# The router's mask, broadcast from its rows on chip, and an earlier transpose in the head of an audio tower

## What is computed

```python
h = gelu(x[:, 1:] @ W[:C] + x[:, :1] @ W[C:] + b)          # [16, 374, 256]
y = layernorm(h)
h = h + y + softmax(y @ y.T / max(|y| |y'|, 1e-8)) @ y      # first norm, "rows 1"
z = layernorm(h)                                            # second norm, "rows 2"
logits = unit(z) @ unit_columns(sim) - sigmoid(gates)       # 8 experts
mask = logits > 0, or the two best experts of a token that has none
w = softmax over the masked experts of relu(logits)
q, k, v = sum_e mask[t, e] * (z @ proj[e])                  # proj: [8, 256, 128] each
a = causal_softmax(q @ k.T / sqrt(128)) @ v
h = h + sum_e mask[t, e] * w[t, e] * (a @ o_proj[e])
```

## Time and profile before

| | |
|---|---|
| median of 3 runs | 699.05 us (698.8 to 699.39) |
| profiled execution | 699.35 us, of which the span from first to last instruction is 697.6 us |
| mean granted TensorE clock | 0.998 |
| PE busy | 681.4 us, 98% |
| DVE busy | 546.7 us, 78% |
| POOL busy | 405.8 us, 58% |
| ACT busy | 345.4 us, 50% |
| DMA | 57.29 MB in 128310 packets, queue q1 35.0% of 16 engines |
| chain that ended last | PE 81%, DVE 6%, issue 5%, POOL 3%, DMA 2%, ACT 2% |

### The profile page before, as it was taken

One profiled execution on the slowest core, in us unless ns is written; L12 is line 12 of the kernel. 1 busy time (PEld: TensorE's weight loads), 2 busy tenths in 40 slices (PEclk: granted clock), 3 DMA queues, 4 the chain that ended last, 5 costly groups with the idle time before them and its releaser, 6 DMA issues.

```text
span 697.6 us, 17459 instructions
## 1 busy us (share of the span) xinstructions
PE 681.4 (98%) x4856; PEld 435.9 (62%) x4856; DVE 546.7 (78%) x1428; ACT 345.4 (50%) x768; POOL 405.8 (58%) x669
## 2 busy tenths in 40 slices
PE   9999989999999999999999999999999999999998
PEld 8887656565655656565655656565655656565555
DVE  5778868786979788796979788796979788786636
ACT  5977444444536354444636354444636354453443
POOL 7552325665747676565747676565747676563534
PEclk9999999999999999999999999999999999999999
DMA  9671142424324252423334242423334242422121
GB/s 247 161 183 50 62 103 43 107 53 90 69 50 112 49 117 49 103 54 87 67 53 112 49 117 46 106 54 86 66 55 112 49 117 45 107 57 68 24 75 31
DMA packets 128310, 57.29 MB, mean 82 GB/s; under 512 B 100264, under 2 KB 124056, under 8 KB 128152
## 3 DMA queue, kind: packets, MB, share of 16 engines
q1 hardware_dynamic: 127888, 56.60, 35.0%
q10 hardware_dynamic: 392, 0.32, 0.1%
HBM read 30.45 MB, written 9.01 MB: 57 GB/s over the span
## 4 chain that ended last, share of the span: by engine, by line
PE 81%; DVE 6%; issue 5%; POOL 3%; DMA 2%; ACT 2%; DVEq 0%; POOLq 0%; ACTq 0%; SPq 0%
PE bank L1820 70%; PE bank L1884 2%; PE bank L1888 2%; PE bank L1886 2%; DVE xm L1407 2%; PE bank L1740 2%; PE bank L1729 1%; DMA mask_all<-d_mask 1%; DMA xT<-xhl 1%; DVE region_b L1290 1%; DMA region_b<-in_x_dram 1%; DVE exp_hl L1428 1%; DVE region_a L1488 1%; POOL small L660 0%; DVE xinT L1211 0%
## 5 line engine op out<-in xcount | busy, mean ns | idle before, releaser
L1820 PE MATMUL bank<-xm,w_qkv 128*128 128x374 f16 x2304 | 409.6, 323 | 0.0
L1820 PEld LDWEIGHTS bank<-xm,w_qkv 128*128 128x128 f16 x2304 | 223.4, 98 | 146.8 <-issue 0.6
L1033 ACT ACTIVATE region_c<-bank,out_w 128x256 f32<-128x256 f32 x180 | 83.3, 473 | 159.1 <-PE bank L1820 142.4
L1820 PE MATMUL bank<-w_o,aoT 128*128 128x512 f16 x540 | 143.1, 379 | 0.4
L1407 DVE TENSOR_TENSOR xm<-xT,mask_all 128x1496 f16<-128x1496 f16 x128 | 139.5, 1103 | 1.5 <-DMA mask_all<-d_mask 1.3
L1312 DVE SCALAR_TENSOR_TENSOR h<-bank,out_w,h 128x256 f32 (+1 forms) x180 | 85.9, 477 | 47.5 <-ACT region_c L1033 45.2
L748 POOL TENSOR_TENSOR region_c<-region_c 128x512 f32<-128x512 f32 x46 | 68.7, 1493 | 25.4 <-ACT region_c L1033 20.5
L787 POOL TENSOR_TENSOR exp_hl<-exp,exp_hl 128x128 f16<-128x128 f32 (+2 forms) x48 | 50.5, 1053 | 56.4 <-ACT exp_hl L976 54.3
L1820 PEld LDWEIGHTS bank<-w_o,aoT 128*128 128x128 f16 x540 | 49.2, 98 | 51.4 <-DVE h L1312 12.9
L755 POOL TENSOR_TENSOR region_c<-region_c 128x256 f32<-128x256 f32 x46 | 47.6, 1034 | 5.8 <-POOL region_c L748 5.5
L902 ACT ACTIVATE aoT<-bank 128x374 f16<-128x374 f32 x15 | 7.2, 483 | 87.7 <-PE bank L1820 87.7
(11 more groups left out here) (211 smaller groups left out, 1026.1 us busy)
## 6 DMA issues: line engine op xcount, KB each, us to landing
mask_all<-d_mask SPq DMA_DIRECT2D x32, 384.0 KB, 4.3
h<-in_x_dram SPq DMA_DIRECT2D x16, 256.0 KB, 4.9
out_dram<-h SPq DMA_DIRECT2D x31, 128.0 KB
rnorm_row<-d_rnorm SPq DMA_DIRECT2D x16, 192.0 KB, 3.6
d_v<-xinT SPq DMA_DIRECT2D x14, 192.0 KB, 4.4
xinT<-d_v SPq DMA_DIRECT2D x56, 48.0 KB, 2.3
h<-in_x_dram SPq DMA_DIRECT2D x15, 112.0 KB, 5.6
out_dram<-h SPq DMA_DIRECT2D x15, 112.0 KB
```

The costliest lines, as they stand in the source:

```text
L1033: a.activation(prod[:, prod_buf(n, t), q, :], pair_bank(n, p)[:, C:2 * C], ACT.Copy, scale=weights_out(n)[:, t, 2 * q + 1:2 * q + 2]).then ...
L1820: last = t_.matmul(dst, left[lp], right[rp], start=(starts and k == 0), stop=(stops and k == 2), skip_group_check=True)
```

## The change

The store of the mask, the wait for it and the two loads go, with their tensor and semaphore. Instead SP issues eight transfers, each of which reads one partition of `maskT` (768 bytes) and writes it to all 128 partitions of `mask_all[:, e, :]`. Four of them count up one semaphore, so that DVE waits for 64 where it waited for 16. ACT, before it overwrites `maskT`, waits for the transfers of the mask before. In the head's last step alone, four orders are changed: on DVE `norm_apply(2)` comes right behind `route(1)`, on ACT `high_1(2)` comes before `turned_mask(1)`, on POOL `low_1(2)` before `route_weights(1)`, and on SP `first_rows_around(2)` comes between `norms_out(2)` and `norms_in(2)`.

```diff
             def mask_around(f):
 
                 sp.wait_ge(s_mask_row, f + 1).then_inc(s_passed, 1)
-                sp.dma_start(d_mask[f, :].rearrange("(e t) -> e t", e=E), maskT[:, :]).then_inc(s_mask_stored, 16)
-                sp.wait_ge(s_mask_stored, 16 * (f + 1)).then_inc(s_passed, 1)
                 if later(f):
                     sp.wait_ge(s_xm_ready, E * f).then_inc(s_passed, 1)
-                for k in range(2):
-                    sp.dma_start(mask_all[:, k * (E // 2):(k + 1) * (E // 2), :].rearrange("p e t -> p (e t)"),
-                                 d_mask[f, k * (E // 2) * TP:(k + 1) * (E // 2) * TP].partition_broadcast(P)).then_inc(
-                                     s_mask_loaded[k], 16)
+                for e in range(E):
+                    sp.dma_start(mask_all[:, e, :], maskT[e:e + 1, :].unsqueeze(1).broadcast_to([1, P, TP])).then_inc(
+                        s_mask_loaded[e // (E // 2)], 16)
...
                 if g is not None:
                     norms_out(g)
+                    if early(m):
+                        first_rows_around(g)
                     norms_in(g)
                 if f is not None and not early(m):
                     mask_around(f)
                 if m is not None and by_trip(m):
                     values_out(m)
-                if g is not None:
+                if g is not None and not early(m):
                     first_rows_around(g)
...
                     row_scales(g1)
+                if early(m):
+                    low_1(g1)
                 if f is not None:
                     route_weights(f)
-                if early(m):
-                    low_1(g1)
...
                 act.wait_ge(s_mask_turned, f + 1)
                 if later(f):
-                    act.wait_ge(s_mask_stored, 16 * f)
+                    for s in s_mask_loaded:
+                        act.wait_ge(s, 16 * (E // 2) * f)
...
                     head_high(qT, qkv_bank[0], s_q_done, m + 1, s_q_hi, [], qkv_out)
+                    high_1(g1)
                     turned_mask(f)
                     route_exp(f)
                     values_out(m)
-                    high_1(g1)
...
                 if e % (E // 2) == 0:
-                    dve.wait_ge(s_mask_loaded[e // (E // 2)], 16 * (b + 1))
+                    dve.wait_ge(s_mask_loaded[e // (E // 2)], 16 * (E // 2) * (b + 1))
...
                     route(f)
+                    norm_apply(0, g1)
                     weights_low(2 * NC)
...
                     turn_values(m)
-                    norm_apply(0, g1)
```

More of the change, by code:

```diff
@@ L166, in audio_tower_kernel @@
         d_v = nc.dram_tensor("d_v", [B, P * TP], F32, kind="Internal").ap()
-        d_mask = nc.dram_tensor("d_mask", [B, E * TP], F16, kind="Internal").ap()
         bank = [ctx.enter_context(nc.psum_tensor(f"bank{i}", [P, 512], F32)) for i in range(8)]
@@ L266, in audio_tower_kernel @@
         s_mask_row = sem("mask_row")
-        s_mask_stored = sem("mask_stored")
         s_mask_loaded = [sem("mask_loaded0"), sem("mask_loaded1")]
```

## The result

The changed kernel takes 1064.9 us (median of 4 runs, 1062.22 to 1067.46) where the kernel before takes 699.22: ratio 1.522, interval 1.517 to 1.528. It is 366 us slower, and not 3.6 faster as forecast.

The account below looks back on a forecast made before the run. TensorE (PE) was taken as otherwise fed, so only its idle places could gain. Head 3.1 + steady steps 0 + tail 0.5 = 3.6 us off 699.35: 695.75 profiled, 695.4 median; range 694.5 to 1120, likeliest case alone 694.5 to 697.3.

Parts of the forecast that it names:

- part 2: Mask in a steady step: eight transfers replace store, wait and two loads; 0.31 us per transfer under 0.46 per issue, no cost.
- 0 in the 13 steady steps: Steady steps neither gain nor lose, as long as one transfer takes at most 0.82 us of the queue.
- The rival of one row for one engine: Mask transfers: one row serves one engine at a time, 4.0 us each, steps 25.6 longer; 1095 to 1120 us; chance 0.36.
- The clock: Slower rival's term: PE's idling lowers its clock each time, 1.5 us, 16 times, raising 1095 to 1120 us at most.
- The estimate worked out from the Trainium skill: Mask transfers: partitions 0 to 3 share one port of about 27.2 GB/s, 3.6 us per transfer, sum about 1065 us.
- The other rivals: Transfers of 1.2 us, 738 us in all, chance 0.08; or head's stall only exchanged, no gain, 698.5 us, chance 0.06.
- Part 1, the head: Head's last step: transposes issued at 90.4, PE's 2.42 us stall and the slow clock behind it go; 3.1 us gained.
- DVE's block before the cosines: Head, DVE from weight_max on: would end at 99.1 to 99.7, wanted at 98.3; taken as 0.3 us late.
- the row-maximum wait of half a microsecond: Head: PE's wait for a row maximum, as in steady steps, was to appear here too, reducing the gain from 3.37 us.
- Part 3, the tail: Tail, batch 15's mask: DVE's 1.34 us wait goes and PE's 0.47 us row-maximum wait with it; 0.5 us gained.

Follow-up runs that it names:

- the probe: Bare kernel that only times DMA series of 768 KB: one partition's row 30.5 us, rows of partitions 0 to 7 in turn 29.1 us.
- the run with the head alone: Changed kernel with the mask again stored to and loaded from memory, the four head orders kept: 696.11 us, ratio 0.995 to the kernel before.
- the run from 128 partitions: Changed kernel, but each of the eight transfers reads 768 bytes from every partition of a constant tile: 696.19 us, ratio 0.996.
- d_own: Series in a bare data-moving kernel: eight 96 KB transfers, every one of 128 partitions reading its own row on chip: 6.5 us.
- e_mem8: Series in a bare data-moving kernel: eight 96 KB transfers of rows from memory to 128 partitions: 6.3 us.
- j_all: Series in a bare data-moving kernel: eight 96 KB transfers from all 128 partitions to memory: 5.1 us.

## Why the forecast was wrong

**The step that failed** is the price of a transfer in part 2 of the prediction: "I take the lower end: the old loads too had all engines read the same 6 KB, from memory, and that is the nearest row." It was nearest in the shape of the access, but not in what limits it. Here memory served one 6 KB row to all engines at 316 GB/s, while a single partition on chip gave 27 GB/s, the rate of the port it stands behind. The transfer cost 3.6 us and not 0.31, eight 29.1 and not the 3.7 of their issue. So "0 in the 13 steady steps" became 23.8 us in each.

**The rival of one row for one engine** had the path of the loss right. Its point of decision, 0.82 us per transfer, was passed by far; its step was 25.6 longer, the measured one 23.8; its sum 1095 to 1120, with 4.0 us per transfer from one engine's best rate. Its mechanism was not exact, since it is not the engine or the row but the port that is taken in turn, and with 3.6 the price is smaller. It also reckoned with one wait, for the transposes, where PE has two. The clock was mis-sized the other way: 1.5 us per round from the head's single stall, 3.7 measured, since in a steady step PE stands idle twice.

The estimate worked out from the Trainium skill, SBUF — State Buffer, section "Door 1: The DMA port swizzle", 1065, is what was measured; the probe's 27 GB/s agrees with the section's 27.2. That it came out to the microsecond is in part luck. The prediction doesn't show its working; by the rival's terms with 3.6 us for a transfer a step is longer by 22.3 for the transposes (28.8 + 3.8, less the 10.3 from the mask to PE's dots before) and 1.5 for the clock, 23.8, and the measured 23.8 is 20.0 of waits and 3.7 of clock. The trace of before held no long read of few partitions, as the forecast said, and in that case the port of that section should have weighed more than a row of another kind of source.

**The other rivals** did not occur: a transfer took 3.6 us and not 1.2, and the head's stall was not exchanged for another, as PE in the run with the head alone waits for nothing from the last units of batch 0 to 142.47.

**Part 1, the head:** right in mechanism and size, in part by luck. 3.1 forecast, 3.7 at the attention products and 3.5 in the median of the run with the head alone; the stall is gone, the clock at its upper level. The transposes were issued at 90.49 where 90.4 was forecast, but not for its reasons. SP had two loads from memory to issue and not eight transfers, and it then waited 1.0 for POOL's low half, which started at 88.68 and not at 87.18, because row_scales ended 1.4 us later than in the kernel before (one instruction of it took 1.48 and not 0.51). With the eight transfers of the run from 128 partitions it is 92.48: an issue costs 0.6 and not 0.46, and nothing is left to spare. DVE's block before the cosines ended at 99.04, about as late as reckoned (99.1 to 99.7), but it cost PE nothing, and the row-maximum wait of half a microsecond that I let reappear did not come either. Against that stands the wait of 1.0 in step 3, which was not in the sum.

**Part 3, the tail:** wrong in size. The run from 128 partitions had the mask early and gained nothing measurable over the head alone, against 0.5 forecast. The idle time of DVE went, but its product took 1.1 us longer.

**Part 2 apart from the price:** "0 in the 13 steady steps" for the issues, the removed store and the moved values holds in the run from 128 partitions to within 1.1 us over all 13 (511.45 from the mask of batch 2 to that of batch 15, against 510.39). With a store's wait kept ahead of the eight issues, as in the run with eight loads from memory, it does not hold.

## What to carry to other kernels

Before a row on chip is broadcast by DMA, count the ports that hold the source, not the engines that read it: here 768 KB from one partition took 30 us, from all 128 it took 4 to 7, and from memory 5 to 6. Where a trace has no row for an access, a row whose shape is like it but whose source is another memory is no bound. And put a price on what stands behind the transfer in the same queue: here half of PE's waits (164.6 us) were for transposes that had nothing to do with the mask.

## What I had not expected of the hardware

The issuing engine was held while its queue could not drain: SP's issue of a transfer took up to 4.0 us in the changed kernel, with a median of 3.1, where the same eight issues with a source in 128 partitions had a median of 0.60. The first two or three of a mask go at that pace, the later ones take about 3.6 each, the time in which one transfer moves. Even unhindered, eight issues on chip took 5 us of SP and not 3.7 (d_own 5.01, 5.05 in a step of the kernel), while eight from memory took 3.69 (e_mem8). The source alone does not decide it: j_all, from all partitions on chip to memory, took 3.69 too.
